# An LSTM recurrence on one core: four of the eight transposes for a coming step are put between the gate products of its two halves

## The chip, the core and the metric

The kernel runs on one core of one Trainium2 chip. The metric is the device time of one execution in microseconds; for the kernel before it is the median of three runs. Five engines run side by side: TensorE (PE in the profile, its weight loads PEld), VectorE (DVE), ScalarE (ACT), GpSimd (POOL) and SyncE (SP, which issues most transfers). They meet only at counters (semaphores): an instruction can wait until a counter has reached a value, and can raise one when it ends.

## The reference

The reference runs a graph convolution with 16 relations, a mixture of 8 experts, a second graph convolution, and an LSTM. Only the LSTM is touched:

```
x_proj = einsum('btd,gd->btg', x, W_ih) + b_ih + b_hh
def step(carry, xp):
    h, c = carry
    gates = xp + h @ W_hh.T
    i, f, g, o = split(gates, 4)
    c = sigmoid(f) * c + sigmoid(i) * tanh(g)
    h = sigmoid(o) * tanh(c)
    return (h, c), h
```

Here there is one sequence of 6,250 rows with 256 features, and a hidden state of 256 values; everything is fp32. Its output is multiplied by 2 and gets sums over the rows before and after each row added to it, at those rows which a small linear layer picks.

## The kernel before

The sequence is cut into 128 pieces (C) of 50 rows (L), which run side by side as 128 columns. A step takes one row of every piece. As a piece needs the state with which the piece before it ends, the steps are run in three passes: a warm-up pass that begins at row 4 (46 steps), and two passes of 50 steps. Between passes `shift` moves every piece's last state to its neighbour. That makes 146 steps, all written out in a straight line. The last pass computes the output as well. The input projections `x_proj` were computed by the stage before and lie in memory as `scratch_xrow`.

**The tiles.** The hidden state is `k_hall`, the input weights' product is already done, and `k_whhT` holds W_hh. The 256 features are in two halves x = 0 and x = 1 of 128. The gates of half x are four blocks of 128 x 128 in one bank of PSUM, `l_psg[:, n % 3, x]`; three steps' banks rotate.

**A turn.** Before step n can begin, its projections must be in the bank. `turn(n)` does that: eight transposes (line 2089) of the block `l_xr`, four for each half. It waits for the transfer that brings `l_xr` (`s_r`) and, as the banks rotate, for `oa` and `ob` (ScalarE has read both halves of step n-3). SP loads the next `l_xr` when both halves of a turn are done (line 2072). Two turns are made ahead, so that `turn(n + 2)` is issued behind step n.

**A step on TensorE** is `step(n, s, h)`, 16 products (line 2096) in `part_of(x, kk, blocks)`, where x is the half of the gates and kk the half of h that is multiplied. The trace has two records for an fp32 product and one for a transpose. The order is: wait for `h0`; (x 0, kk 0) four products; (x 1, kk 0) two (`EARLY`); wait for `h1`; (x 0, kk 1) four, which end with `ma`; (x 1, kk 0) the other two; (x 1, kk 1) four, which end with `mb`. Then `turn(n + 2)`, and in the last pass `Out.rows` (line 1921, two products) for the output.

**Behind it.** `ma` releases ScalarE's activations of half 0 (lines 2143 to 2145); VectorE forms the cell (2172, 2174, 2176), ScalarE its tanh (2150), and VectorE the new state (2181), which raises `h0` for the next step. `mb` does the same for half 1: 2152 to 2154, then 2172, 2174, 2176, tanh 2156, then 2181, which raises `h1`. Both engines keep the order in which the code is written: all of half 0 up to its tanh stands ahead of 2152 on ScalarE, and 2181 of half 0 ahead of 2172 of half 1 on VectorE. In the last pass ScalarE has 1940 and 1932 and VectorE 1949 to 1989 as well, for the output.

Of the kernel before, what the change touches and what calls it, by code (L numbers as in the profile page):

```python
# [1871 lines left out]
def stage_lstm(k, W_lin, b_lin, fw, bw, out):  # L1872
# [10 lines left out]
    with ExitStack() as st:  # L1883
# [172 lines left out]
        def sweep(passes, opening):  # L2056

            total = sum(L - f for f, _ in passes)
            starts = [sum(L - f for f, _ in passes[:a]) for a in range(len(passes))]
            order = [s for f, _ in passes for s in range(f, L)]  # L2060
            with nc.Block(no_gpsimd_drain=True) as block:
                @block.sync
                def _(sp):
                    if opening:
                        sp.dma_start(wl[:], W_lin).then_inc(S["ld"], 16)
                        sp.dma_start(bl[:], b_lin.partition_broadcast(P)).then_inc(S["ld"], 16)
                        sp.dma_start(dif[:], fw.rearrange("a d -> (a d)").partition_broadcast(P)).then_inc(S["ld"], 16)
                        sp.dma_start(bwb[:], bw.rearrange("a d -> (a d)").partition_broadcast(P)).then_inc(S["ld"], 16)
                    for n, s in enumerate(order):
                        if n >= RING:  # L2070
                            sp.wait_ge(S["tt"], 2 * (n - RING) + 2)
                        sp.dma_start(xr[:, n % RING].rearrange("p g c -> p (g c)"), xrow[s]).then_inc(s_r[n % RING], 16)
                        if opening and n and n % 8 == 0 and n // 8 <= L // 10:
                            a = 10 * (n // 8 - 1)
                            sp.dma_start(k.x3s[:, a:a + 10], x3[:, a:a + 10]).then_inc(S["x3"], 16)

                    if opening:
                        Out.store(sp)

                @block.tensor  # L2080
                def _(pe):
                    def turn(n):
                        pe.wait_ge(s_r[n % RING], 16 * (n // RING + 1))
                        if n >= 3:
                            pe.wait_ge(S["oa"], n - 2)
                            pe.wait_ge(S["ob"], n - 2)
                        for x in range(2):
                            for g in range(4):
                                mm = pe.matmul(psg[:, n % 3, x, g * C:(g + 1) * C], xr[:, n % RING, 4 * x + g], k.ident[:],  # L2089
                                               start=(g == 0), stop=(g == 3), is_transpose=True, skip_group_check=True)  # L2090
                            mm.then_inc(S["tt"], 1)

                    def step(n, s, h):
                        def part_of(x, kk, blocks):
                            for g in blocks:
                                mm = pe.matmul(psg[:, n % 3, x, g * C:(g + 1) * C], k.whhT[:, kk, 4 * x + g], k.hall[:, s, kk],  # L2096
                                               start=False, stop=(kk == 1), skip_group_check=True)
                            return mm

                        pe.wait_ge(S["h0"], h)  # L2100
                        part_of(0, 0, range(4))
                        part_of(1, 0, range(EARLY))
                        pe.wait_ge(S["h1"], h)
                        part_of(0, 1, range(4)).then_inc(S["ma"], 1)
                        part_of(1, 0, range(EARLY, 4))
                        part_of(1, 1, range(4)).then_inc(S["mb"], 1)

                    turn(0)
                    turn(1)
                    if opening:  # L2110
                        pe.wait_ge(S["ld"], 64)
                        for kk in range(2):
                            mm = pe.transpose(psh[:, 0, kk * 2:kk * 2 + 2], wl[:, kk * P:(kk + 1) * P], k.ident[0:2, 0:2])
                        mm.then_inc(S["wt"], 1)
                    for a, (first, shifted) in enumerate(passes):
                        h0 = 1 + sum(1 for _, f in passes[:a + 1] if f)
                        for s in range(first, L):
                            n = starts[a] + s - first
                            step(n, s, n + h0)
                            if n + 2 < total:  # L2120
                                turn(n + 2)
                            if opening and a == len(passes) - 1:
                                if s == 0:
                                    pe.wait_ge(S["cs"], 8)
                                else:
                                    Out.rows(pe, s - 1)
                    if opening:
                        for h in ("h0", "h1"):
                            pe.wait_ge(S[h], total + 1 + sum(1 for _, f in passes if f))
                        Out.rows(pe, L - 1)  # L2130
                        Out.totals(pe)
                        pe.wait_ge(S["q"], 6)
                        pe.matmul(psh[0:1, 0, 0:1], oks[:, 0:1], k.ones[:, 0:1], start=True, stop=True).then_inc(S["pe"], 1)
# [31 lines left out]
                def _(v):  # L2165
# [59 lines left out]
                    for a, (first, shifted) in enumerate(passes):  # L2225
                        if opening and a == len(passes) - 1:
                            v.wait_ge(S["x3"], 16 * (L // 10))
                        if shifted:
                            if a:
                                v.wait_ge(S["h1"], starts[a] + 1 + sum(1 for _, f in passes[:a] if f))  # L2230
                            shift()
                        for s in range(first, L):
                            n = starts[a] + s - first
                            if opening and n == 1:
                                v.wait_ge(S["wt"], 1)
                                for kk in range(2):
                                    v.tensor_copy(rows_of[:, kk, (P if kk == 0 else 0):(P if kk == 0 else 0) + 2],
                                                  psh[:, 0, kk * 2:kk * 2 + 2]).then_inc(S["cs"], 1)
                                    v.tensor_copy(rows_of[:, kk, 2 * kk:2 * kk + P], k.ident[:]).then_inc(S["cs"], 1)
                                v.tensor_scalar(nbw[:], bwb[:], -1.0, None, ALU.mult).then_inc(S["cs"], 1)  # L2240
                                v.tensor_tensor(dif[:], dif[:], bwb[:], ALU.subtract).then_inc(S["cs"], 1)
                                v.wait_ge(S["cs"], 8)
                            step(n, s, opening and a == len(passes) - 1)
                    if opening:
                        Out.before(v, L - 2)
                        output(L)
                        Out.before(v, L - 1)
                        output(L + 1)
                        Out.ends(v)
                        TOTAL = float(2 * 2 * (CU - 1) * P)  # L2250
                        v.wait_ge(S["h1"], total + 1 + sum(1 for _, f in passes if f))
                        link = Chain(v, S["q"])
                        link(v.tensor_tensor(moved[:, 0], k.hall[:, L, :, 0:CU - 1], k.hall[:, 0, :, 1:CU], ALU.subtract))
                        for x in range(2):
                            link(v.tensor_tensor(moved[:, 1, x], gate[x][:, 0, 0:CU - 1], cell0[:, x, 1:CU], ALU.subtract))
                        link(v.tensor_tensor(moved[:], moved[:], moved[:], ALU.mult))
                        link(v.tensor_scalar(moved[:], moved[:], TOL * TOL, None, ALU.is_le))
                        link(v.tensor_reduce(oks[:, 0:1], moved[:].rearrange("p a k c -> p (a k c)"), AX, ALU.add))
                        v.wait_ge(S["pe"], 1)
                        link(v.tensor_scalar(okf[:], psh[0:1, 0, 0:1], TOTAL - 0.5, None, ALU.is_lt))  # L2260
                        link(v.tensor_copy(flag[:], okf[:]))
# [123 lines left out]
```

## Time and profile before

| | |
|---|---|
| median of 3 runs | 4183.59 us (4181.93 to 4184.46) |
| the profiled execution | 4178.51 us, its span 4176.8 us |
| mean granted TensorE clock | 0.898 |
| the recurrence's first product to its last | 3437.3 to 4134.0 us of the span |
| products of the recurrence (line 2096) | 4672 records, 567.1 us busy |
| transposes of the turns (line 2089) | 1168 records |

The times of the trace are microseconds from the span's start. Records of TensorE overlap (each is shown with its whole way through the array), so the distance between starts tells its pace, not the length of a record.

### The profile page before, as it was taken

The numbers are of one execution on the slowest core, as the hardware profiler recorded it, in microseconds if no ns is written. First come the engines' busy times: TensorE is split into PE (matmuls) and PEld (weight loads), VectorE is DVE, ScalarE is ACT, GpSimd is POOL, SyncE is SP. The second block draws the span as 40 slices with busy tenths as digits, with TensorE's granted clock in tenths as the row PEclk, the third lists the DMA queues.
The fourth block names the chain that finished last, engine by engine and source line by source line (L and its number), as shares of the span: only waits on it lengthen the run. The fifth ranks groups of instructions, "written<-read, shape, count | busy, mean of one in ns | idle before, by whom it ended". The sixth has DMA issues, their size and how long they took to land. (4 is left out here: it accounts for less than half of the span.)

```text
span 4176.8 us, 61028 instructions
## 1 busy us (share of the span) xinstructions
PE 3518.3 (84%) x19585; PEld 2719.4 (65%) x19585; DVE 1860.8 (45%) x5745; ACT 871.1 (21%) x2377; POOL 1660.0 (40%) x1756
## 2 busy tenths in 40 slices
PE   6999999787888888869999366666778879999996
PEld 3444444477777778846666155555556559999996
DVE  4555400133445556643333722233445544444687
ACT  2333333200000011112222500000000004444453
POOL 2000000277777777731010577777777740000000
PEclk9999999878878888879999567888988999999998
DMA  4333444333444444532221643444455554433333
GB/s 145 150 146 149 145 180 168 141 111 113 119 121 133 135 127 141 153 111 68 62 81 56 204 134 110 120 130 141 145 153 163 167 160 151 141 108 116 107 107 108
DMA packets 224592, 544.84 MB, mean 130 GB/s; under 512 B 44195, under 2 KB 125350, under 8 KB 210447
## 3 DMA queue, kind: packets, MB, share of 16 engines
q1 hardware_dynamic: 139744, 314.86, 22.2%
q0 software_dynamic: 80768, 220.83, 18.7%
q10 hardware_dynamic: 3760, 5.24, 0.4%
q8 instruction: 156, 2.56, 0.3%
q14 instruction: 164, 1.34, 0.1%
HBM read 363.60 MB, written 176.74 MB: 129 GB/s over the span
## 5 line engine op out<-in xcount | busy, mean ns | idle before, releaser
L1671 POOL DMA_INDIRECT b_msg<-scratch_gtab,k_src_row x784 | 761.7, 972 | 257.2 <-issue 249.6
L909 POOL DMA_INDIRECT a_msg<-scratch_hrel,k_rel_row x784 | 759.3, 968 | 241.7 <-issue 233.1
L1720 PE MATMUL b_ps<-b_hit,b_msg 128*128 128x128 f32 x3136 | 484.0, 319 | 281.5 <-DMA b_msg<-scratch_gtab,k_src_row 271.6
L703 PE MATMUL r_psm<-k_w,r_xnT 128*128 128x512 f32 x1568 | 692.3, 596 | 5.1 <-ACT r_hst L667 4.2
L1720 PEld LDWEIGHTS b_ps<-b_hit,b_msg 128*128 128x128 f32 x3136 | 452.3, 229 | 353.7 <-issue 275.8
L975 PE MATMUL a_ps<-a_hit,a_msg 128*128 128x128 f32 x3136 | 508.6, 329 | 138.1 <-DMA a_msg<-scratch_hrel,k_rel_row 136.1
L975 PEld LDWEIGHTS a_ps<-a_hit,a_msg 128*128 128x128 f32 x3136 | 469.6, 237 | 169.3 <-issue 91.5
L2096 PE MATMUL l_psg<-k_hall,k_whhT 128*128 128x128 f32 x4672 | 567.1, 279 | 5.7 <-DVE k_hall L2213 5.4
L2096 PEld LDWEIGHTS l_psg<-k_hall,k_whhT 128*128 128x128 f32 x4672 | 544.4, 193 | 13.5 <-DVE k_hall L2213 5.9
L703 PEld LDWEIGHTS r_psm<-k_w,r_xnT 128*128 128x128 f32 x1568 | 292.8, 191 | 348.3 <-issue 340.1
L667 ACT COPY r_hst<-r_psm 128x512 f32<-128x512 f32 x392 | 229.3, 586 | 469.9 <-PE r_psm L703 469.2
L1809 DVE TENSOR_TENSOR k_accT<-k_accT,b_ps 128x256 f32 x196 | 82.6, 422 | 529.4 <-PE b_ps L1720 518.3
L898 POOL MEMSET g_xn<- 128x128 f32 x1 | 0.2, 209 | 755.3 <-issue 755.3
L1097 DVE SCALAR_TENSOR_TENSOR a_hit<-k_iota,k_rel,a_psw 128x128 f32<-128x128 f32 x784 | 219.0, 339 | 114.0 <-PE a_psw L962 113.4
L962 PE MATMUL a_psw<-k_degT,a_hotT 16*128 x1568 | 252.9, 306 | 19.1 <-DMA g_bias<-in_L_gnn_W_b_dram 16.6
L962 PEld LDWEIGHTS a_psw<-k_degT,a_hotT 16*128 16x128 f32 x1568 | 213.1, 207 | 56.6 <-issue 49.2
L1107 DVE TENSOR_TENSOR k_accT<-k_accT,a_ps 128x256 f32 x196 | 82.6, 421 | 363.5 <-PE a_ps L975 329.4
L1344 PE MATMUL x_psy<-x_w2s,x_hT 128*128 128x256 f32 x1024 | 230.4, 379 | 0.0
L1332 PE MATMUL x_psh<-x_xT,x_w1s 128*128 128x465 f32 (+1 forms) x512 | 213.5, 578 | 0.3 <-ACT x_b1T L1355 0.3
L1344 PEld LDWEIGHTS x_psy<-x_w2s,x_hT 128*128 128x128 f32 x1024 | 190.7, 190 | 26.7 <-issue 3.2
L1747 PE MATMUL n_psm<-n_wT,n_xT 128*128 128x512 f32 x392 | 196.0, 625 | 0.5 <-ACT n_xT L1779 0.5
L1424 POOL DMA_INDIRECT x_xr<-scratch_xtab,k_slot_token x64 | 61.8, 966 | 305.0 <-ACT x_yg L1372 241.3
(272 smaller groups left out, 3626.2 us busy)
## 6 DMA issues: line engine op xcount, KB each, us to landing
scratch_hrel<-r_hst SPq DMA_DIRECT2D x98, 1024.0 KB
l_xr<-scratch_xrow SPq DMA_DIRECT2D x146, 512.0 KB, 3.6
scratch_xrow<-n_xs SPq DMA_DIRECT2D x50, 512.0 KB, 3.1
a_msg<-scratch_hrel,k_rel_row POOLq DMA_INDIRECT x784, 2.8
b_msg<-scratch_gtab,k_src_row POOLq DMA_INDIRECT x784, 2.8
scratch_ybuf<-x_ys SPq DMA_DIRECT2D x7, 1024.0 KB, 13.4
scratch_xtab<-g_xn SPq DMA_DIRECT2D x49, 132.0 KB, 3.2
scratch_x<-n_xo SPq DMA_DIRECT2D x50, 128.0 KB, 3.6
```

What stands on the lines that cost most here:

```text
L667: act.copy(hst[:, u, c * 512:(c + 1) * 512], psm[:, c % 4]).then_inc(S["ea"], 1)
L703: mm = pe.matmul(psm[:, c % 4], xnT[:, u, kk], k.w[:, kk, c * 512:(c + 1) * 512], start=(kk == 0), stop=(kk == 1))
L909: pool.indirect_dma_start(msg[:, q, j], None, table, bass.IndirectOffsetOnAxis(ap=rows_of[:, g, j:j + 1].bitcast(U32), axis=0)).then_inc(s ...
L962: mm = pe.matmul(psw[:, u, j * P:(j + 1) * P], hotT[:, u, j * P:(j + 1) * P], k.degT[:, bass.ds(at, WIN)], start=True, stop=True)
L975: mm = pe.matmul(ps[:, u, kk, 0:WIN], msg[:, g % SL, j, kk * P:(kk + 1) * P], hit[:, u, j], start=(j == 0), stop=(j == PER - 1))
L1097: ins = v.scalar_tensor_tensor(out=hit[:, u, j], in0=k.iota[:], scalar=k.rel[:, g, j:j + 1], in1=psw[:, u, j * P:(j + 1) * P], op0=ALU.is_ ...
L1332: mm = pe.matmul(psh[:, i % 4, 0:z - a], w1s[:, u, kk, f * P:(f + 1) * P], xT[:, u, kk, a:z], start=(kk == 0), stop=(kk == 1))
L1344: mm = pe.matmul(psy[:, n % 2, 0:D], hT[:, f, n * P:(n + 1) * P], w2s[:, u, f], start=(f == 0), stop=(f == FB - 1))
L1671: pool.indirect_dma_start(msg[:, q, j], None, k.gtab, bass.IndirectOffsetOnAxis(ap=k.src_row[:, g, j:j + 1].bitcast(U32), axis=0)).then_in ...
L1720: mm = pe.matmul(ps[:, u, kk, 0:WIN], msg[:, g % SL, j, kk * P:(kk + 1) * P], hit[:, u, j], start=(j == 0), stop=(j == PER - 1))
L1747: mm = pe.matmul(psm[:, h], xT[:, t % 2, kk], wT[:, kk, 4 * h:4 * h + 4].rearrange("p g d -> p (g d)"), start=(kk == 0), stop=(kk == 1))
L2096: mm = pe.matmul(psg[:, n % 3, x, g * C:(g + 1) * C], k.whhT[:, kk, 4 * x + g], k.hall[:, s, kk], start=False, stop=(kk == 1), skip_group_ ...
```

## The change

The turn of step n + 2 is cut in two by halves. `turn` takes the halves that it is to make; the four transposes of half 0 are issued inside step n, between the products that end with `ma` and the rest of the products of half 1, and the four of half 1 where all eight stood. The two turns ahead of the first step are made whole as before. Every turn after them now waits twice for the transfer, `oa` and `ob`: once at each of its parts. Nothing else is changed, and no transfer or operation is added or removed.

```diff
-                    def turn(n):
+                    def turn(n, half):
                         pe.wait_ge(s_r[n % RING], 16 * (n // RING + 1))
                         if n >= 3:
                             pe.wait_ge(S["oa"], n - 2)
                             pe.wait_ge(S["ob"], n - 2)
-                        for x in range(2):
+                        for x in half:
...
                         part_of(1, 0, range(EARLY))
                         pe.wait_ge(S["h1"], h)
                         part_of(0, 1, range(4)).then_inc(S["ma"], 1)
+                        if n + 2 < total:
+                            turn(n + 2, (0,))
                         part_of(1, 0, range(EARLY, 4))
                         part_of(1, 1, range(4)).then_inc(S["mb"], 1)
 
-                    turn(0)
-                    turn(1)
+                    turn(0, (0, 1))
+                    turn(1, (0, 1))
...
                             step(n, s, n + h0)
                             if n + 2 < total:
-                                turn(n + 2)
+                                turn(n + 2, (1,))
```

TensorE's order in the program of before, at the second step of the first pass. A product counts once here. The counters go by the name of their first holder: `g_pe` is `h0` and `g_sl` is `h1`; `g_nm`, `g_rec` are `ob` and `oa`, and `g_ld`, `g_x0`, `g_x1` the three transfers.

```order
L2096 MATMUL l_psg<-k_hall,k_whhT 128x128 [waits g_pe]
L2096 MATMUL l_psg<-k_hall,k_whhT 128x128 x5
L2096 MATMUL l_psg<-k_hall,k_whhT 128x128 [waits g_sl]
L2096 MATMUL l_psg<-k_hall,k_whhT 128x128 x9
L2089 MATMUL l_psg<-k_ident,l_xr 128x128 [waits g_nm,g_rec,g_ld]
L2089 MATMUL l_psg<-k_ident,l_xr 128x128 x7
```

The same step in the program of the change:

```order
L2096 MATMUL l_psg<-k_hall,k_whhT 128x128 [waits g_pe]
L2096 MATMUL l_psg<-k_hall,k_whhT 128x128 x5
L2096 MATMUL l_psg<-k_hall,k_whhT 128x128 [waits g_sl]
L2096 MATMUL l_psg<-k_hall,k_whhT 128x128 x3
L2089 MATMUL l_psg<-k_ident,l_xr 128x128 [waits g_nm,g_rec,g_ld]
L2089 MATMUL l_psg<-k_ident,l_xr 128x128 x3
L2096 MATMUL l_psg<-k_hall,k_whhT 128x128 x6
L2089 MATMUL l_psg<-k_ident,l_xr 128x128 [waits g_nm,g_rec,g_ld]
L2089 MATMUL l_psg<-k_ident,l_xr 128x128 x3
```

Between the wait for `h1` and the end of the gates of half 1 stood ten products; now four transposes stand among them, and four are left behind them.

TensorE's order in the last pass, before. Line 1921 is the output's two products, and `g_s6` a counter that only they wait for.

```order
L2096 MATMUL l_psg<-k_hall,k_whhT 128x128 [waits g_pe]
L2096 MATMUL l_psg<-k_hall,k_whhT 128x128 x5
L2096 MATMUL l_psg<-k_hall,k_whhT 128x128 [waits g_sl]
L2096 MATMUL l_psg<-k_hall,k_whhT 128x128 x9
L2089 MATMUL l_psg<-k_ident,l_xr 128x128 [waits g_nm,g_rec,g_x1]
L2089 MATMUL l_psg<-k_ident,l_xr 128x128 x7
L1921 MATMUL l_psh<-l_rows_of,k_hall 128x130 [waits g_s6]
L1921 MATMUL l_psh<-l_rows_of,k_hall 128x130
```

And in the program of the change:

```order
L2096 MATMUL l_psg<-k_hall,k_whhT 128x128 [waits g_pe]
L2096 MATMUL l_psg<-k_hall,k_whhT 128x128 x5
L2096 MATMUL l_psg<-k_hall,k_whhT 128x128 [waits g_sl]
L2096 MATMUL l_psg<-k_hall,k_whhT 128x128 x3
L2089 MATMUL l_psg<-k_ident,l_xr 128x128 [waits g_nm,g_rec,g_x1]
L2089 MATMUL l_psg<-k_ident,l_xr 128x128 x3
L2096 MATMUL l_psg<-k_hall,k_whhT 128x128 x6
L2089 MATMUL l_psg<-k_ident,l_xr 128x128 [waits g_nm,g_rec,g_x1]
L2089 MATMUL l_psg<-k_ident,l_xr 128x128 x3
L1921 MATMUL l_psh<-l_rows_of,k_hall 128x130 [waits g_s6]
L1921 MATMUL l_psh<-l_rows_of,k_hall 128x130
```

The move is the same; behind the four that are left the output's two products still follow.

## Rows read from the trace of the kernel before

**Rows 1.** The profile's page, its first line.

```profile
span 4176.8 us, 61028 instructions
```

**Rows 2.** Busy time by windows: stretch, each engine's busy us (instructions), clock, DMA share, GB/s.

```profile
3440.00:3640.00 200.00, 200.00 (x1732) 196.66 (x1732) 93.54 (x353) 84.26 (x348) 0.00 (x0) 1.00 0.47 148
3900.00:4130.00 230.00, 230.00 (x2069) 229.91 (x2067) 186.95 (x701) 126.43 (x471) 0.00 (x0) 1.00 0.35 102
```

**Rows 3.** Waits of the recurrence, 3434 to 4135: us in total, times, longest.

```profile
ACT l_gate L2143 <- PE l_psg L2096: 249.9, 146, 12.8
...
PE l_psg L2096 <- DVE k_hall L2213: 5.4, 2, 2.8
```

**Rows 4.** Timeline, pass 1: start, us, engine, line, [idle before <-releaser].

```profile
3524.18 0.91 PEld L2089 LDWEIGHTS l_psg<-k_ident,l_xr 128*128 128x128 f32 x8
...
3524.76 0.29 DVE L2181 TENSOR_TENSOR k_hall<-l_gate,l_tc 128x128 f32<-128x128 f32 x1 [0.38 <-ACT l_tc L2150]
...
3525.11 3.77 PEld L2096 LDWEIGHTS l_psg<-k_hall,k_whhT 128*128 128x128 f32 x32
...
3526.22 0.29 DVE L2181 TENSOR_TENSOR k_hall<-l_gate,l_tc 128x128 f32<-128x128 f32 x1 [0.38 <-ACT l_tc L2156]
3527.77 0.38 ACT L2143 ACTIVATE l_gate<-l_psg 128x256 f32<-128x256 f32 x1 [1.57 <-PE l_psg L2096]
...
3528.80 0.91 PEld L2089 LDWEIGHTS l_psg<-k_ident,l_xr 128*128 128x128 f32 x8
...
3529.04 0.31 ACT L2150 ACTIVATE l_tc<-l_gate 128x128 f32<-128x128 f32 x1 [0.55 <-DVE l_gate L2176]
3529.25 0.37 ACT L2152 ACTIVATE l_gate<-l_psg 128x256 f32<-128x256 f32 x1
3529.38 0.29 DVE L2181 TENSOR_TENSOR k_hall<-l_gate,l_tc 128x128 f32<-128x128 f32 x1 [0.38 <-ACT l_tc L2150]
...
3530.85 0.29 DVE L2181 TENSOR_TENSOR k_hall<-l_gate,l_tc 128x128 f32<-128x128 f32 x1 [0.38 <-ACT l_tc L2156]
```

**Rows 5.** Timeline of PEld alone, 3526.53 to 3526.6: the first load behind `h1`.

```profile
3526.57 0.19 PEld L2096 LDWEIGHTS l_psg<-k_hall,k_whhT 128*128 128x128 f32 x1
```

**Rows 6.** Timeline at the end of pass 1, and ScalarE's line 2152 in 3524.3:3649.0 (busy, mean ns).

```profile
3648.99 0.91 PEld L2089 LDWEIGHTS l_psg<-k_ident,l_xr 128*128 128x128 f32 x8
...
L2152 ACT ACTIVATE l_gate<-l_psg 128x256 f32<-128x256 f32 x27 | 9.9, 368 | 0.0
```

**Rows 7.** Timeline of the steps behind the two pass boundaries.

```profile
3652.82 6.60 PEld L2096 LDWEIGHTS l_psg<-k_hall,k_whhT 128*128 128x128 f32 x32 [2.92 <-DVE k_hall L2213]
...
3659.34 0.91 PEld L2089 LDWEIGHTS l_psg<-k_ident,l_xr 128*128 128x128 f32 x8
...
3659.65 0.38 ACT L2152 ACTIVATE l_gate<-l_psg 128x256 f32<-128x256 f32 x1 [0.57 <-PE l_psg L2096]
...
3889.66 5.47 PE L2096 MATMUL l_psg<-k_hall,k_whhT 128*128 128x128 f32 x32 [2.76 <-DVE k_hall L2213]
```

**Rows 8.** Timeline, last pass.

```profile
4086.65 3.65 PEld L2096 LDWEIGHTS l_psg<-k_hall,k_whhT 128*128 128x128 f32 x32
...
4090.22 0.91 PEld L2089 LDWEIGHTS l_psg<-k_ident,l_xr 128*128 128x128 f32 x8
...
4090.68 0.37 ACT L2152 ACTIVATE l_gate<-l_psg 128x256 f32<-128x256 f32 x1
...
4092.27 0.29 DVE L2181 TENSOR_TENSOR k_hall<-l_gate,l_tc 128x128 f32<-128x128 f32 x1
...
4094.50 0.29 DVE L2172 TENSOR_TENSOR l_part<-l_gate 128x128 f32<-128x128 f32 x1 [0.40 <-ACT l_gate L2143]
...
4096.44 3.65 PEld L2096 LDWEIGHTS l_psg<-k_hall,k_whhT 128*128 128x128 f32 x32
```

**Rows 9.** The page's DMA issues: KB each, median us from issue to landing.

```profile
l_xr<-scratch_xrow SPq DMA_DIRECT2D x146, 512.0 KB, 3.6
```

## The prediction

> **What bounds the kernel now.** The page gives a span of 4176.8 us [rows 1]. The change touches the recurrence alone, so I read its three passes first by windows, then by waits, then step by step. By windows TensorE is busy for 200 of 200 us in pass 1 and 230 of 230 in the last pass, at the full 2.4 GHz clock (granted 1.00) [rows 2]; and the waits show ScalarE waiting for the products, 249.9 us in 146 waits, while TensorE waits long only twice, at the pass boundaries [rows 3]. Read so, TensorE alone sets the pace, and the order of its work within a step could not matter. The reader should distrust this: a matmul's record covers its way through the array, so stalls shorter than a record vanish under the one before. Starts have to be compared.
>
> In the last pass the 32 product loads of a step take 3.65 us [rows 8], in pass 1 they take 3.77 [rows 4]: 0.12 us are lost inside the step. Of 0.19 us each, they start (3.65 - 0.19)/31 = 0.112 apart. The 12 records ahead of the h1 wait take 1.34 us, so TensorE, which began at 3525.11 [rows 4], was ready for h1 at 3526.45, and went on at 3526.57 [rows 5]. State 1 was written from 3526.22 for 0.29 [rows 4], so 0.06 us after its end TensorE goes on: this is the h1 wait. The other one is at h0: state 0 ends at 3524.76 + 0.29 = 3525.05 and the step begins at 3525.11 [rows 4], while eight transposes at 0.11 from 3524.18 would have let it begin at 3525.06. So 0.05 and 0.12 us, 0.17 per step, are waits; a step takes (3648.99 - 3524.18)/27 = 4.62 us [rows 4, 6], and TensorE's own work 4.45.
>
> So passes 1 and 2 are bound by a loop, not by TensorE. From the h1 release, which I call G (3526.57), it goes to 2143 at 3527.77 (1.20), to the tanh 2150 at 3529.04 (1.27), to 2152 behind it at 3529.25 (0.21), to state 1 at 3530.85 (1.60), and from state 1's start to the next G 0.35 (3526.22 to 3526.57) [rows 4, 5]. Together 4.63; measured 4.62. A second branch goes by mb: from G to the first transpose, whose load starts when the last product does, 2.23 (3526.57 to 3528.80) [rows 4, 5]; from there 2152 could begin after 0.31, as at the one place where it waits for the products alone (3659.34 to 3659.65) [rows 7]. Here it begins after 0.45 [rows 4], since half 0's tanh stands ahead of it. The mb branch takes 2.23 + 0.31 + 1.60 + 0.35 = 4.49 us: it has 0.14 us to spare, and no more.
>
> The last pass has four more records behind the transposes. Its step takes (4096.44 - 4086.65)/2 = 4.895 us [rows 8], and TensorE does bind it: h1 is ready at 4092.27 + 0.29 + 0.06 = 4092.62. The step in the middle of these two begins at 4091.55, and TensorE comes to h1 1.34 later, at 4092.89, which leaves 0.27.
>
> **The change, part by part.** It removes and adds no operation. It moves four transposes from behind mb to ahead of it. Eight take 0.91 with a last of 0.14, so they start 0.11 apart, and four are worth 0.44 us. ma is issued ahead of them and isn't moved, so all of half 0 keeps its times; and between ma and the next step as much lies on TensorE as before, so h0 keeps its 0.05. mb ends 0.44 later relative to G. Of this 0.14 is hidden under 2150, so 2152 begins 0.30 later, and behind it on ScalarE 2153, 2154 and the tanh 2156, on VectorE the three cell operations and state 1 with them. Nobody else waits for these in passes 1 and 2; TensorE does, at h1, and there it already waits today, so nothing covers the 0.30.
>
> The mb branch is then 2.23 + 0.44 + 0.31 + 1.60 + 0.35 = 4.93 us, which is above 4.62: plus 0.30 (0.31 by this sum; 0.30 by 0.44 less the cover). It counts for the 96 steps of passes 1 and 2, the two ahead of the shifts among them, since shift waits for state 1 of the last step; 96 x 0.30 = 28.8 us. The first step of the last pass has no output products behind it: another 0.3.
>
> In the other steps of the last pass the same branch is 2.23 + 0.44 + 0.31 + 1.59 (4090.68 to 4092.27 [rows 8]) + 0.35 = 4.92, against 4.895 that TensorE needs: 0.025 per step in the 47 steps but the last two, which have no turn: 45 x 0.025 = 1.1 us. The rows allow 0 to 0.045 here, 0 to 2.0 us. The output's operations on VectorE begin 0.3 later too; it idles 0.40 ahead of half 0's next 2172 [rows 8], so they still end in time.
>
> The turn's second set of waits I cost at nothing: the state reads behind oa and ob are of the step before and end well ahead of G, and the transfer takes 3.6 us [rows 9] against a lead of nearly three steps, some 13 us, of which the early half loses 12 records, 1.34 us. The next transfer is issued when half 1 is done, as now. For the wait instruction itself the nearest row is the 0.06 us from a state to TensorE; if every one of the 144 cost that much, 8.6 us. I take zero, since the present turn starts with the same wait and its load follows at the usual distance (from G to it 20 records in 2.23 us, 0.112 each).
>
> The boundaries are the last part. TensorE idles there 2.92 and 2.76 us and the clock falls to 1.2 GHz: the next step's loads take 6.60 us instead of 3.77, and at the second boundary its matmuls 5.47 [rows 7], about 1.6 above the usual. TensorE will idle 0.3 longer. Where the low stretch ends is a matter of chance: both like the first is plus 1.2, both like the second minus 1.2, none at all minus 4.4. I take zero.
>
> Sum: 28.8 + 0.3 + 1.1 = 30.2 us. On the profiled execution's 4178.5 that is 4208.7. It was 5.1 us quicker than the median of the runs shown, so on 4183.6 it is 4213.8, plus 0.72%.
>
> **A rule weighed against the rows.** The turns run at 1.00 clock beside the products, and passes 1 and 2 had no fall of it but at the boundaries [rows 2, 7]. The Trainium skill, "TensorE: Matmul & The Clock Gate", Part 4, says that the full clock does not engage for matmuls in transpose mode. By the rows the sum stays as above; by the rule, four transposes amid the products and a longer stall behind them could let the clock fall within the passes. No trace here shows a step with transposes in its middle.
>
> **Rivals.** (a) The clock falls within passes 1 and 2: products, transposes, then 0.4 us of stall in every step. A step at the low clock costs 6.60 - 3.77 = 2.8 us more [rows 7]; one fall per 20 steps makes 14 us, 4228, and if all 96 ran low it would be 270 us more. Against it: stalls of 0.17 per step leave 1.00, and known falls come behind idle stretches of almost 3 us. (b) The move is hidden: half 1's chain has more to spare than I find, and the loop stays at 4.62; 4184. It would need 0.44 of cover, and the rows show 0.14. (c) It is faster. The chain of half 1 (2152 to state 1) runs beside the transposes' writes to PSUM; were it slowed by these, halving their number there would shorten it. It decides above 0.30 us off 1.60, and if both waits vanished, TensorE's 4.45 would bind: 96 x 0.17 = 16 us less, 4167. Against it: half 0's chain, which runs beside products only, takes 1.61 (3527.77 to 3529.38) [rows 4], no less. (d) Half of it: ScalarE or VectorE have shorter paths when they come to half 1 idle, and 0.15 is left: 4199.
>
> **How the numbers follow.** My forecast, a stall of 0.27 to 0.33 per step, gets 0.84; (a) 0.04; (b) 0.04; (c) 0.03; (d) 0.05. The range takes in 0.28 x 97 without the last pass and with 1.2 less at the boundaries, minus 1.3 for the spread of the runs (4183.6 + 24.7, rounded down to 4207), and upward 0.31 x 97 + 2.0 + 1.2 + 1.3, and a third of the wait instructions' bound (4183.6 + 37.5 = 4221). 0.2% is 8.4 us, about what measuring this kernel can tell from no change. Slower by more: forecast, (a) and (d), 0.93. Within: (b), 0.04. Faster: (c), 0.03.
>
> **What the trace of the changed kernel would show.** The first transpose load behind G after 0.89 us; 2152 with its own wait for the products in every step (today it shows none in passes 1 and 2); turn to turn 4.92 us there; 2143 and state 0 unmoved against G; TensorE stalled about 0.4 us at h1 and 0.05 at h0; the last pass at 4.90 to 4.94; clock 1.00 between the boundaries. I am wrong if 2152 still starts right behind 2150, if 1.60 becomes shorter, or if other stages move by more than 3 us.

## The result, and the profile after

| | before | changed |
|---|---|---|
| median of 4 runs | 4184.02 us | 4213.95 us (4211.27 to 4216.78) |
| ratio | 1 | 1.0074, 95% interval 1.0061 to 1.0087 |
| the profiled execution | 4178.51 us | 4216.78 us |

The change makes the kernel 0.74% slower, 29.9 us between the medians; the interval allows 25.5 to 36.4 us. The forecast was 4213.8 us. In the changed kernel all lines behind line 2096 are two higher: 2143 is 2145 there, 2150 is 2152, 2152 is 2154, 2156 is 2158 and 2181 is 2183.

First the busy time by windows, in pass 2 and in the last pass, with the columns of [rows 2]:

```profile
3700.00:3900.00 200.00, 193.13 (x1625) 184.50 (x1624) 86.94 (x325) 83.55 (x324) 0.00 (x0) 1.00 0.37 109
3940.00:4170.00 230.00, 229.85 (x2052) 229.66 (x2050) 186.81 (x698) 131.14 (x468) 0.00 (x0) 1.00 0.34 102
```

In pass 2 TensorE has still no more than 7 us of idle time in 200, but its load unit has 15.5. The granted clock is 1.00, as it was. The waits of the recurrence, which answer to [rows 3]:

```profile
PEld l_psg L2096 <- DVE k_hall L2183: 34.2, 96, 0.4
ACT l_gate L2154 <- PE l_psg L2096: 27.9, 142, 0.2
PE l_psg L2096 <- DVE k_hall L2183: 15.6, 93, 0.2
...
PE l_psg L2096 <- DVE k_hall L2215: 6.1, 2, 3.1
```

Two waits are new. TensorE's loads wait for the state (line 2183) in 96 cases, 34.2 us, and ScalarE's first activation of half 1 (2154) now waits for the products in 142 cases of 146. Before, the same list had one case of the first (0.4 us) and two of the second (1.1 us). The timeline of one step of pass 1 and the start of the next, beside [rows 4]:

```profile
3524.10 0.97 PEld L2096 LDWEIGHTS l_psg<-k_hall,k_whhT 128*128 128x128 f32 x8 [0.36 <-DVE k_hall L2183]
...
3524.99 0.47 PEld L2089 LDWEIGHTS l_psg<-k_ident,l_xr 128*128 128x128 f32 x4
...
3525.30 0.38 ACT L2145 ACTIVATE l_gate<-l_psg 128x256 f32<-128x256 f32 x1 [1.57 <-PE l_psg L2096]
...
3526.57 0.31 ACT L2152 ACTIVATE l_tc<-l_gate 128x128 f32<-128x128 f32 x1 [0.55 <-DVE l_gate L2178]
3526.76 0.47 PEld L2089 LDWEIGHTS l_psg<-k_ident,l_xr 128*128 128x128 f32 x4
...
3527.07 0.39 ACT L2154 ACTIVATE l_gate<-l_psg 128x256 f32<-128x256 f32 x1 [0.19 <-PE l_psg L2096]
3527.26 1.42 PEld L2096 LDWEIGHTS l_psg<-k_hall,k_whhT 128*128 128x128 f32 x12
...
3528.68 0.29 DVE L2183 TENSOR_TENSOR k_hall<-l_gate,l_tc 128x128 f32<-128x128 f32 x1 [0.38 <-ACT l_tc L2158]
3529.03 0.97 PEld L2096 LDWEIGHTS l_psg<-k_hall,k_whhT 128*128 128x128 f32 x8 [0.35 <-DVE k_hall L2183]
```

Read it from the first row, the release by h1 (the prediction's G). Half 0 is where it was against G: 2145 at +1.20 and the tanh 2152 at +2.47, both as in [rows 4, 5]. The second group of transposes, whose first load starts when the last product of half 1 does, begins at +2.66 instead of +2.23, and 2154 follows 0.31 later, released by the products and no longer held by the tanh. It is 1.77 behind 2145, where it was 1.48 behind it. State 1 is written 1.61 after that, the next G follows 0.35 later: 2.66 + 0.31 + 1.61 + 0.35 = 4.93 us, and 3524.10 to 3529.03 is 4.93.

In the last pass the step takes 4133.28 - 4128.35 = 4.93 us, against 4.895 [rows 8]:

```profile
4128.35 0.47 PEld L2089 LDWEIGHTS l_psg<-k_ident,l_xr 128*128 128x128 f32 x4
4128.79 1.42 PEld L2096 LDWEIGHTS l_psg<-k_hall,k_whhT 128*128 128x128 f32 x12
4130.13 0.47 PEld L2089 LDWEIGHTS l_psg<-k_ident,l_xr 128*128 128x128 f32 x4
4130.57 0.53 PEld L1921 LDWEIGHTS l_psh<-l_rows_of,k_hall 128*128 128x128 f32 x4
4131.02 2.35 PEld L2096 LDWEIGHTS l_psg<-k_hall,k_whhT 128*128 128x128 f32 x20
4133.28 0.47 PEld L2089 LDWEIGHTS l_psg<-k_ident,l_xr 128*128 128x128 f32 x4
```

No idle time is shown here, and a step is still longer: the 20 loads from 4131.02 on contain the wait for h1, 0.04 us, too short to be listed.

By stretches, from the first activation of half 0 in a pass to that of its last step (it starts at 3439.88, 3647.96; 3657.50, 3884.72; 3893.01, 4132.97 before; 3451.44, 3673.12; 3682.26, 3923.70; 3931.47, 4172.72 after):

| | before | after | difference |
|---|---|---|---|
| pass 1 | 208.08 | 221.68 | +13.60 |
| first boundary | 9.54 | 9.14 | -0.40 |
| pass 2 | 227.22 | 241.44 | +14.22 |
| second boundary | 8.29 | 7.77 | -0.52 |
| last pass | 239.96 | 241.25 | +1.29 |

That is 28.2 us; from the recurrence's first product to its last it is 28.6 (3437.3 to 4134.0 before, 3448.5 to 4173.8 after: 696.7 and 725.3). The two profiled spans lie 38.2 apart: 11.2 of this came before the first product, in stages whose instructions are the same, and 1.6 was won back behind the recurrence. What is known of these 11.2 stands under "What was said too firmly".

### The profile page after: what moved, and what is told of

Its sections match the earlier page's. It is cut to its first block and busy times, and to the rows that moved or that the text cites. A ratio compares the mean times of both kernels' runs of the same rounds, so it can differ in the third digit from the quotient of the medians.

```text
span 4215.0 us, 61171 instructions
## 1 busy us (share of the span) xinstructions
PE 3535.2 (84%) x19585; PEld 2723.9 (65%) x19585; DVE 1862.0 (44%) x5745; ACT 887.9 (21%) x2377; POOL 1669.0 (40%) x1756
## 5 line engine op out<-in xcount | busy, mean ns | idle before, releaser
L2096 PE MATMUL l_psg<-k_hall,k_whhT 128*128 128x128 f32 x4672 | 602.8, 279 | 22.0 <-DVE k_hall L2183 15.6
L2096 PEld LDWEIGHTS l_psg<-k_hall,k_whhT 128*128 128x128 f32 x4672 | 554.6, 192 | 43.0 <-DVE k_hall L2183 34.2
L2089 PE MATMUL l_psg<-k_ident,l_xr 128*128 128x128 f32 x1168 | 176.5, 275 | 13.9 <-DMA l_xr<-scratch_xrow 13.9
```

## Experiments

All are made from the kernel before unless it is said otherwise, and each was profiled once. Fifteen executions of the kernel before took 4175.41 to 4185.86 us, so a single time can't tell effects of a few us apart; the length of a step in the profile is the measure. In the experiments that move transposes, the turn takes a list of blocks (half, gate):

```diff
-                    def turn(n):
+                    def turn(n, blocks):
...
-                        for x in range(2):
-                            for g in range(4):
-                                mm = pe.matmul(...)
-                            mm.then_inc(S["tt"], 1)
+                        for x, g in blocks:
+                            mm = pe.matmul(...)
+                            if g == 3:
+                                mm.then_inc(S["tt"], 1)
```

### How much the middle holds: none, one, two, all eight

Behind the products that end with `ma` stands `turn(n + 2, MID)`, and at the end of the step `turn(n + 2, REST)`. MID is empty, one, two, or all eight blocks. Here with one; with all eight the turn at the end of the step is left out, and with it the second set of waits:

```diff
                         part_of(0, 1, range(4)).then_inc(S["ma"], 1)
+                        if n + 2 < total:
+                            turn(n + 2, MID)
...
-                    turn(0)
-                    turn(1)
+                    WHOLE = [(0, 0), (0, 1), (0, 2), (0, 3), (1, 0), (1, 1), (1, 2), (1, 3)]
+                    MID, REST = [(0, 0)], [(0, 1), (0, 2), (0, 3), (1, 0), (1, 1), (1, 2), (1, 3)]
+                    turn(0, WHOLE)
+                    turn(1, WHOLE)
...
-                                turn(n + 2)
+                                turn(n + 2, REST)
```

With an empty MID (`mid_waits`), only the second set of waits is left in the middle:

> All eight transposes at the end as before, and only the second set of waits (transfer, oa, ob) in the middle of the step. My loop: nothing changes, 4.62 us in passes 1 and 2 and 4.89 in the last. Rival by the waits: up to 4.93 in passes 1 and 2; with the nearest row's 0.06 for a wait, 4.68 and 4.95.

One block (`mid_one`):

> One transpose (half 0's first) between the products that end with ma and the rest of half 1's, seven at the end. My loop: the branch through mb has 0.14 us to spare and one transpose is worth 0.11, so a step of passes 1 and 2 stays at 4.62 us (branch 4.60) and the last pass at 4.89; line 2152's group is held by the tanh ahead of it for 0.03 only. A rival without cover, in which each transpose costs its share of the 0.30 measured (0.075), gives 4.70. A rival in which the second set of waits makes the cost gives 4.93.

Two blocks (`mid_two`):

> Two transposes in the middle, six at the end. My loop: 4.49 + 0.22 = 4.71 us per step in passes 1 and 2, 0.08 above before, 4.89 in the last pass (its loop of 4.71 lies below TensorE's own work); about 8 us in all. Rival without cover: 4.77. Rival by the waits: 4.93.

All eight (`mid_all`):

> All eight transposes in the middle, none at the end. My loop: 4.49 + 0.87 = 5.36 us per step in all three passes, so 0.74 more in passes 1 and 2 and 0.47 in the last: 97 x 0.74 + 45 x 0.47 = 93 us. Rival without cover, 0.075 each: 5.22 in passes 1 and 2. Rival by the waits alone (one set of waits per step, as before): 4.62.

Measured, as timelines of ScalarE alone in pass 1: the first activation of each half, in two steps that follow one another. In these files half 0's is line 2147 and half 1's 2156 (2145 and 2154 with all eight). The waits alone:

```profile
3554.23 0.38 ACT L2147 ACTIVATE l_gate<-l_psg 128x256 f32<-128x256 f32 x1 [1.57 <-PE l_psg L2096]
...
3555.72 0.37 ACT L2156 ACTIVATE l_gate<-l_psg 128x256 f32<-128x256 f32 x1
...
3558.86 0.38 ACT L2147 ACTIVATE l_gate<-l_psg 128x256 f32<-128x256 f32 x1 [1.57 <-PE l_psg L2096]
```

One block:

```profile
3551.34 0.38 ACT L2147 ACTIVATE l_gate<-l_psg 128x256 f32<-128x256 f32 x1 [1.57 <-PE l_psg L2096]
...
3552.83 0.37 ACT L2156 ACTIVATE l_gate<-l_psg 128x256 f32<-128x256 f32 x1
...
3555.97 0.38 ACT L2147 ACTIVATE l_gate<-l_psg 128x256 f32<-128x256 f32 x1 [1.57 <-PE l_psg L2096]
```

Two blocks:

```profile
3552.69 0.38 ACT L2147 ACTIVATE l_gate<-l_psg 128x256 f32<-128x256 f32 x1 [1.57 <-PE l_psg L2096]
...
3554.25 0.38 ACT L2156 ACTIVATE l_gate<-l_psg 128x256 f32<-128x256 f32 x1
...
3557.40 0.38 ACT L2147 ACTIVATE l_gate<-l_psg 128x256 f32<-128x256 f32 x1 [1.57 <-PE l_psg L2096]
```

All eight:

```profile
3550.60 0.39 ACT L2145 ACTIVATE l_gate<-l_psg 128x256 f32<-128x256 f32 x1 [1.58 <-PE l_psg L2096]
...
3552.81 0.38 ACT L2154 ACTIVATE l_gate<-l_psg 128x256 f32<-128x256 f32 x1 [0.63 <-PE l_psg L2096]
...
3555.96 0.38 ACT L2145 ACTIVATE l_gate<-l_psg 128x256 f32<-128x256 f32 x1 [1.57 <-PE l_psg L2096]
```

| transposes between ma and mb | mb branch, 4.49 + 0.11 each | step, passes 1 and 2 | half 1 behind half 0 | step, last pass | time, one execution |
|---|---|---|---|---|---|
| 0 (before) | 4.49 | 4.62 | 1.48 | 4.895 | 4185.08 |
| 0, with the waits | 4.49 | 4.62 | 1.49 | 4.89 | 4179.67 |
| 1 | 4.60 | 4.62 | 1.49 | 4.89 | 4179.64 |
| 2 | 4.71 | 4.71 | 1.56 | 4.89 | 4193.42 |
| 4 (the change) | 4.93 | 4.93 | 1.77 | 4.93 | 4216.78 |
| 8 | 5.36 | 5.37 | 2.21 | 5.37 | 4279.69 |

The 4185.08 us of the kernel before are from its one execution on the chip of the four experiments; that of the change is the profiled one. Means over 42 steps of pass 1 are 4.621, 4.622, 4.711 and 5.367 us for the four. So the step is the longer of 4.62 and the mb branch, in the last pass the longer of 4.89 and the same branch. The first transpose is free, the second costs 0.09, and from there each costs its whole 0.11. That refutes the cost without cover (0.075 each from the first on) and the cost by the waits: with the waits alone nothing moves.

Busy time with all eight in the middle, in pass 1 and in the last pass:

```profile
3460.00:3660.00 200.00, 177.52 (x1495) 170.48 (x1494) 80.63 (x300) 76.67 (x298) 0.00 (x0) 1.00 0.42 131
4000.00:4200.00 200.00, 192.33 (x1644) 185.30 (x1642) 150.14 (x559) 104.86 (x374) 0.00 (x0) 1.00 0.34 99
```

Eight transposes amid the products and, in each step, 0.8 us without a load in pass 1 leave the granted clock at 1.00, which is 2.4 GHz.

### Half 1's transposes in the middle

MID is `[(1, 0), (1, 1), (1, 2), (1, 3)]`, REST the four of half 0.

> The change with the halves swapped: half 1's four transposes in the middle, half 0's at the end. My loop knows only how late mb comes, so 4.93 us per step in all passes, as with half 0's. A rival in which the cost comes from which bank is written beside which activation's read makes it differ from 4.93 by more than 0.03.

```profile
3551.12 0.38 ACT L2147 ACTIVATE l_gate<-l_psg 128x256 f32<-128x256 f32 x1 [1.57 <-PE l_psg L2096]
...
3552.89 0.39 ACT L2156 ACTIVATE l_gate<-l_psg 128x256 f32<-128x256 f32 x1 [0.20 <-PE l_psg L2096]
...
3556.05 0.38 ACT L2147 ACTIVATE l_gate<-l_psg 128x256 f32<-128x256 f32 x1 [1.57 <-PE l_psg L2096]
```

4.93 us per step, 1.77 between the halves, 4215.42 us in one execution: the same as the change. No part of the cost is seen to hang on which bank the transposes write.

### Half 0's transposes ahead of the wait for h1

MID is half 0's four blocks, REST half 1's.

```diff
                         part_of(0, 0, range(4))
                         part_of(1, 0, range(EARLY))
+                        if n + 2 < total:
+                            turn(n + 2, MID)
                         pe.wait_ge(S["h1"], h)
```

> Half 0's four transposes ahead of the wait for h1 instead of behind ma. TensorE then comes to the h1 wait 1.34 + 0.44 = 1.78 us behind the step's start, later than h1, so the wait for h1 vanishes, and half 0's own loop binds: 1.78 + 0.89 to the last product of ma + 2.27 from there to the next step = 4.94 us, in all passes. 2152 is again held by the tanh and starts 1.48 behind 2143, where the change has 1.78; TensorE waits at h0, about 0.5 per step in passes 1 and 2. A rival in which transposes cost only between ma and mb gives 4.62.

```profile
3553.07 1.41 PEld L2096 LDWEIGHTS l_psg<-k_hall,k_whhT 128*128 128x128 f32 x12 [0.46 <-DVE k_hall L2185]
...
3554.40 0.47 PEld L2088 LDWEIGHTS l_psg<-k_ident,l_xr 128*128 128x128 f32 x4
...
3554.84 2.31 PEld L2096 LDWEIGHTS l_psg<-k_hall,k_whhT 128*128 128x128 f32 x20
...
3558.00 1.41 PEld L2096 LDWEIGHTS l_psg<-k_hall,k_whhT 128*128 128x128 f32 x12 [0.46 <-DVE k_hall L2185]
```

4.93 us per step as well (3553.07 to 3558.00), and 4216.12 us; but by the other loop. The wait of 0.46 us is now at the step's start, for h0, and the 20 loads behind the transposes take 2.31 us, without any wait for h1. Half 1's first activation is 1.49 behind half 0's, held by the tanh as before. So transposes cost here too, since they delay ma instead of mb.

### One product less, before and after

Here a piece of work is left out: the last product of half 1 with kk 0, so that the fourth gate block of half 1 lacks half of its sum. It is ahead of mb and behind ma.

```diff
-                        part_of(1, 0, range(EARLY, 4))
+                        part_of(1, 0, range(EARLY, 3))
```

In the kernel before (`less_before`):

> The kernel before with one of its 16 products left out, the last one of half 1 with kk 0 (so the fourth gate of half 1 lacks half its sum): mb comes 0.22 us earlier and TensorE has 0.22 less to do. My loop: 4.62 us in passes 1 and 2, unchanged, and 4.67 in the last pass, which TensorE binds; 11 us in all. If TensorE bound passes 1 and 2 as its busy time says, 4.40 there and 33 us in all.

In the changed kernel (`less_after`):

> The changed kernel with the same product left out. My loop: mb binds, so 4.93 - 0.22 = 4.71 us in all three passes. A rival in which the change's cost doesn't go by way of mb (the wait for h1 or the waits' place) leaves 4.93.

Loads of `less_before` in pass 1, then in the last pass:

```profile
3550.57 3.55 PEld L2096 LDWEIGHTS l_psg<-k_hall,k_whhT 128*128 128x128 f32 x30 [0.24 <-DVE k_hall L2181]
3554.04 0.91 PEld L2089 LDWEIGHTS l_psg<-k_ident,l_xr 128*128 128x128 f32 x8
3555.19 3.55 PEld L2096 LDWEIGHTS l_psg<-k_hall,k_whhT 128*128 128x128 f32 x30 [0.24 <-DVE k_hall L2181]
...
4050.73 3.43 PEld L2096 LDWEIGHTS l_psg<-k_hall,k_whhT 128*128 128x128 f32 x30
...
4055.40 3.43 PEld L2096 LDWEIGHTS l_psg<-k_hall,k_whhT 128*128 128x128 f32 x30
```

In pass 1 a step still takes 4.62 us (3550.57 to 3555.19). TensorE has 0.22 less to do, and its loads stand idle for 0.24 at the step's start, where [rows 4] list none, the wait of 0.05 there being too short; the 0.12 at h1 is still there (3.55 against 3.43 in the last pass). In the last pass the step is 4.67, 0.22 shorter: there TensorE binds. The changed kernel without the product:

```profile
3550.59 0.38 ACT L2145 ACTIVATE l_gate<-l_psg 128x256 f32<-128x256 f32 x1 [1.57 <-PE l_psg L2096]
...
3552.14 0.38 ACT L2154 ACTIVATE l_gate<-l_psg 128x256 f32<-128x256 f32 x1
...
3555.29 0.38 ACT L2145 ACTIVATE l_gate<-l_psg 128x256 f32<-128x256 f32 x1 [1.57 <-PE l_psg L2096]
```

4.70 to 4.71 us per step, 0.22 shorter. The same product is worth nothing in passes 1 and 2 of before, and its whole length in the changed kernel. One execution each took 4168.02 and 4184.58 us, the kernel before 4179.33 on the same chip.

### A shorter boundary

None of the places tried above is better for the transposes than the end of the step. The boundaries offered something: TensorE needs only the moved hidden state, and `shift` moves the cell state first.

```diff
                     def shift():
+                        for x in range(2):
+                            v.tensor_copy(k.hall[:, 0, x, 1:C], k.hall[:, L, x, 0:C - 1]).then_inc(S[f"h{x}"], 1)
                         for x in range(2):
                             moves(v.tensor_copy(cell0[:, x, 1:C], gate[x][:, 0, 0:C - 1]))
                         moves(v.memset(cell0[:, :, 0:1], 0.0))
                         for x in range(2):
                             moves(v.tensor_copy(gate[x][:, 0], cell0[:, x]))
-                        for x in range(2):
-                            v.tensor_copy(k.hall[:, 0, x, 1:C], k.hall[:, L, x, 0:C - 1]).then_inc(S[f"h{x}"], 1)
```

> The kernel before, with the hidden state moved first in the shift between two passes and the cell state behind it. TensorE needs only the hidden state, so each of the two boundaries is about 1.2 us shorter (3651.37 to 3652.54 lay ahead of it), 2.3 us in all; if the shorter idle time also keeps the clock at its full level, up to 4.4 more. Per step nothing changes, 4.62 and 4.89. A rival in which the cell state is needed as early: 0.

The first boundary in its timeline:

```profile
3655.72 0.36 DVE L2208 COPY k_hall<-k_hall 128x127 f32<-128x127 f32 x2
...
3656.01 3.65 PEld L2096 LDWEIGHTS l_psg<-k_hall,k_whhT 128*128 128x128 f32 x32 [1.75 <-DVE k_hall L2208]
```

TensorE idles 1.75 us there instead of 2.92, 1.17 less, and the next step's loads take 3.65 us instead of 6.60 [rows 7]: the clock did not fall. From first product to last the recurrence took 3441.7 to 4131.7, 690.0 us, 6.7 less than before. Part of this is chance of the clock: `mid_waits` and `mid_one`, with steps as long as before's, took 695.0 and 693.9 us. Over 11 executions against 15 of before the median is 4176.89 against 4179.90 us, ratio 0.9991 with an interval of 0.9982 to 1.0000. It points to about 3 us, and the interval reaches to no change; it is no more than likely that it beats before.

## Why the prediction was right

**The bound.** That pass 1 is bound by a loop and not by TensorE, though it is busy 200 of 200 us, is shown by the product left out: 0.22 us of TensorE's work gone, step unchanged. That the last pass is bound by TensorE is shown by the same experiment. The load unit's column in [rows 2] already hinted at it: 196.66 us of 200 in pass 1, against 229.91 of 230 in the last pass.

**The 0.14 us to spare.** One transpose was free, two cost 0.09, four cost 0.30. With 0.11 for each this puts the cover between 0.13 and 0.14.

**The path by mb.** 2154 waits for the products in 142 steps; the same transposes in another bank cost the same; with a product less ahead of mb the changed kernel gives 0.22 back. Half 0 did not move against G.

**Nothing for the second waits.** Shown by the waits alone: 4.62 and 4.89.

**Sizes.** A step of passes 1 and 2 was forecast 0.30 longer and is 0.305 (4.622 to 4.927, means over 42 steps of pass 1). In the last pass 0.025 was forecast and 0.035 came. I had kept the 1.59 us from the activation to state 1, as it was when the activation did not wait; in the timeline after, where it waits, it takes 1.62 (4130.44 to 4132.06). With the measured sizes the steps give 97 x 0.305 + 45 x 0.035 = 31.2 us.

The term that was mis-sized is the clock at the boundaries, which I took as zero between a bound of plus 1.2 and one of minus 4.4. The step behind the first boundary took 7.50 us before and 5.98 after, from its start to the next one's, and that behind the second 6.18 and 4.59: 3.1 us less. Both are taken by the starts of matmuls. The windows show the granted clock at the beginning of these steps (1.00 is full; it is the figure behind the busy times), first in the kernel before, then in the changed one, each at the first and the second boundary:

```profile
3652.80:3656.60 3.80, 3.78 (x17) 3.78 (x18) 0.10 (x1) 0.00 (x0) 0.00 (x0) 0.50 0.05 22
3889.70:3893.50 3.80, 3.80 (x24) 3.80 (x25) 0.11 (x2) 0.49 (x3) 0.00 (x0) 0.69 0.06 18
...
3678.30:3682.10 3.80, 3.80 (x21) 3.80 (x22) 0.07 (x1) 0.00 (x0) 0.00 (x0) 0.60 0.00 1
3928.90:3932.70 3.80, 3.76 (x33) 3.77 (x34) 0.89 (x4) 0.72 (x3) 0.00 (x0) 1.00 0.01 3
```

The very first step took 0.3 more (4.56 before, 4.87 after), as its first products ran at a granted clock of 0.50 (3448.60 to 3449.20). 31.2 - 3.1 + 0.3 = 28.4, and 28.6 was measured.

**Luck.** The forecast lies 0.15 us from the measured median, which is closer than it deserves: the interval of the difference is 25.5 to 36.4 us, and in the profiles the forecast's 30.2 stands against 28.6, since the boundaries gave back what the steps cost beyond it and more. The mechanism rests on the steps, not on this hit.

**What was said too firmly.** That other stages would not move by more than 3 us; by that sign the prediction would have been wrong. In eleven profiles of this study, whose stages ahead of the recurrence have the same instructions, the first product comes between 3437.3 us (before) and 3448.5 (after); the others lie between, as `less_before` at 3439.6 and `mid_two` at 3446.5. The lag of the changed kernel builds up along the way: at the same matmul it is 0.9 us behind at 255 us of the span, 3.1 at 1319 and 5.2 at 2010. That this is a scatter between executions, and not something which the change does to the stages ahead, is likely but not shown: every kernel was profiled once. For it speak that 15 executions of one kernel spread over 10.5 us, that the profiled execution of before was shorter than each of its four timed ones and that of the change the longest of its four, and that the medians lie 29.9 apart, only 1.3 more than the recurrence's 28.6. So the 38.2 us between the two profiled spans are not taken as the change's size; the distance inside the recurrence is.

**The rivals.** (a), a fall of the clock within the passes: not in the change, and not with eight transposes in the middle and 0.8 us of stall. For the Trainium skill's rule ("TensorE: Matmul & The Clock Gate", Part 4) that the full clock does not engage in transpose mode, the windows of that kernel are the measure: 1.00 in both, so it does not hold here, where products stand around the transposes. A longer stretch of transposes alone is in none of these windows. (b), a hidden move: true for one transpose, not for four. (c), faster by less interference in PSUM: the chain of half 1 did not become shorter with half the transposes beside it, 1.61 us against 1.60. (d), shorter paths when the engines come idle: none appeared.

## What to carry to other kernels

In a recurrence, measure a step from start to start, and walk every loop from one release back to itself: the longest is the step, the next ones say how much each piece of work may be late. Work without a deadline belongs behind the last signal that somebody waits for; between two signals it is free only up to the slack of the second. That an engine is busy for the whole stretch does not say that it binds: here a removed product was worth nothing until the order made it count.

## What was unexpected of the hardware

At a pass boundary almost the same idle time of TensorE had different results. The prediction's 2.92 and 2.76 us [rows 7] can't be compared with each other, as the first is idle time of the loads and the second of the matmuls. By timelines of TensorE's matmuls alone, the kernel before at its first boundary:

```profile
3652.82 6.79 PE L2096 MATMUL l_psg<-k_hall,k_whhT 128*128 128x128 f32 x32 [2.68 <-DVE k_hall L2213]
```

`mid_one` at its first:

```profile
3657.90 2.50 PE L2096 MATMUL l_psg<-k_hall,k_whhT 128*128 128x128 f32 x20 [2.69 <-DVE k_hall L2217]
```

And the changed kernel at its first and second boundary:

```profile
3678.29 3.93 PE L2096 MATMUL l_psg<-k_hall,k_whhT 128*128 128x128 f32 x20 [2.99 <-DVE k_hall L2215]
...
3928.94 2.50 PE L2096 MATMUL l_psg<-k_hall,k_whhT 128*128 128x128 f32 x20 [3.06 <-DVE k_hall L2215]
```

20 records took 2.50 us twice and 3.93 once, with almost equal idle time ahead of them; and behind 2.68 us of it the step of the kernel before was slow (32 records in 6.79 us), behind 2.69 that of `mid_one` was not. In the eleven profiles there are 22 boundaries. The granted clock fell at 17 of them, with 2.68 to 3.50 us of idle time, and stayed at 1.00 at five: both of `hall_first` (1.51 and 1.57), the first of `mid_one` (2.69) and of `mid_two` (2.78), and the second of the changed kernel (3.06). So between 2.68 and 3.06 us the length alone does not decide; what does, these runs don't show.
